# Attention's chain with one more fill point ahead of the latent, the scores and the last transposes; odd chunks 42 points behind even ones

## The chip, the cores and the metric

The kernel runs on one core of one Trainium2 chip. The metric is the device time of one execution in microseconds. Three runs of the kernel before gave 2309.78, 2309.92 and 2310.56 us; their median is 2309.92 us. A measurement of this kernel can tell a change of about 0.2%, some 4.6 us, from none.

## What is computed

Two layers over x of 8 sequences x 1024 tokens x 512 features, in float32, each with a layer norm ahead and a residual behind:

```python
x = x + attention(layernorm(x))
x = x + ffn(layernorm(x))

# attention
kv_latent = x @ W_to_kv.T                 # 512 -> 128
c  = kv_latent @ W_compress.T             # 128 -> 64
ch = layernorm(c) * gamma + beta
q  = rope(ch @ W_q.T);  k, v = split(ch @ W_kv.T);  k = rope(k)
o  = softmax(causal(q @ k.T / 8)) @ v     # one head of 64
z  = o @ W_comp2lat.T
out = z @ W_to_kv + z @ W_out_res.T + b

# ffn
hidden = silu(x @ W1.T) * (x @ W3.T)      # 512 -> 2048
out = fwht(hidden) @ W2.T                 # Walsh-Hadamard, 2048 -> 512
```

## The kernel before

**Tiling.** A sequence is cut into two chunks of 512 tokens; chunks are numbered a = 0 to 15, the even one is the first half of a sequence. A chunk has four tiles of 128 tokens. Every product is made of high and low parts (float16 or rounded float32), hence pairs and triples of matmuls. The attention of the two first chunks is done ahead of the main loop, in an order written out by hand.

**Main loop.** It runs over k = 0 to 127: sequence s = k // 16 and block h = k % 16 of the feed-forward's hidden features. Each k has seven products i = 0 to 6 of six matmuls each (`product`, L767 to L769; a seven-product scheme for the 2x2 block product). Behind products 1, 3, 5 and 6 TensorE does a `down` step (L791 to L793, six matmuls) for the second feed-forward matmul of four blocks before. VectorE and ScalarE turn the seven products into the hidden features: `copy_b` (ScalarE, behind product 0), `copy_p5` (behind 1), `sum_c` (VectorE, behind 2, needs copy_p5), `silu` 0 (ScalarE, behind 3), `sum_e` (VectorE, behind 4), `silu` 1 (behind 5), `hidden` 1 (VectorE, behind silu 1), `hidden` 0 (behind product 6 and silu 0), `high` (ScalarE, behind both hidden) and `low_part` (VectorE). Product (k, 2) waits for copy_b, (k, 4) for sum_c, (k, 6) for sum_e, (k+1, 1) for hidden 1. ScalarE does high(k-1) ahead of copy_b(k). `out_rows` (VectorE) takes a finished down tile to the output rows.

**Fill points.** While sequence s goes through the feed-forward, the attention of sequence s + 1 is laid into the same loop. After each product (and its down step) is a fill point f = 7h + j, j = 0 to 6. There every engine asks `SLOTS.get(f)`, which names the slot that each of the two chunks is at: the even chunk's slot is f - 3, the odd one's f - 3 - `ODD`. Each engine has a function `attention(a, slot)` that does its part of the slot. Every engine runs in its own order of instructions, so what stands in front of an attention step on an engine delays it, and the step delays what stands behind. Where a step falls among the engine's own work of the block is set by j: on ScalarE, point 0 lies between copy_b and copy_p5, 1 and 2 between copy_p5 and silu 0, 3 and 4 between the two silus, 5 and 6 behind silu 1 and ahead of high; on VectorE, 0 and 1 lie behind low_part of the block before and ahead of out_rows and sum_c, 2 and 3 between sum_c and sum_e, 4 ahead of hidden 1, 5 and 6 behind it and out_rows and ahead of hidden 0 (in every fourth block point 6 goes behind hidden 0 and high).

**The slots of a chunk before.** 0 to 3: `conv` (ScalarE L939, VectorE L1393) splits a block of x transposed; SP loads two more. 1 to 4: `cproj` on TensorE (L502, L503), the compression products; their source has one buffer, so conv and cproj go in turn. 5: `latent`: ScalarE copies the product (L945), TensorE turns it (L515), ScalarE copies the result (L951). 6: `squares`. 7, 8: statistics of x. 9 to 11: `norm1`, its Newton steps, `norm1_parts` (V, L1437). 13: `values`. 14: `proj`. 14 to 17: `rope`, ending with Q (L1475). From slot `TILE0` = 18 on come four tiles, 6 slots apart in an even chunk and 8 in an odd one: `scores` (L556) and `maxima` at +0, `exps` (ScalarE, L983, and its copies to high, L988) at +1, `low` (VectorE, L1496) at +2, transposes (L571, copied out by ScalarE, L999) at +4, `pv` (L586) at +5, `outp` (L596) one or two later, VectorE's part of it at +7. An odd chunk's tiles have 5 to 8 blocks of 128 keys, an even one's 1 to 4. Behind the last tile (`end_slot`): `norm2` at +1, `norm2_root` (nine small Newton operations, L1364 to L1368) at +2, `xnorm` from +3 and `xtrans` (L605, copied out by L1009) from +4.

`exps` needs another function table on ScalarE than `silu`; an ACT_TABLE_LOAD stands ahead of each change.

Two PSUM banks, X and Y, serve all attention steps of both chunks. In sequence 0 the loop carries more: the W1 and W3 forms are scaled and split (`scale_rows` on bank Y, L728; `forms_high` on ScalarE; `forms_low`), W2 is transformed (`hadamard2`, L719; `split2`), and there are no down steps in the first four blocks. `SCALE_AT` sets the points of scale_rows, moved by one where `y_held` says that a tile holds Y. SP issues loads and stores at fixed points and at slots: `load_x` at slot 3, the next chunk's `load_xT` at slot 36.

Of the kernel before, what the change touches and what calls it, by code (L numbers as in the profile page):

```python
# [16 lines left out]
NC = 16  # L17
# [22 lines left out]

ODD = 41
TILE0 = 18
NSLOT = 57
SLOTS = {z + 3: [(c, z - ODD * c) for c in range(2) if 0 <= z - ODD * c < NSLOT] for z in range(ODD + NSLOT)}


def y_held(f):

    return any(slot - TILE0 in ((0, 8, 16, 24) if c else (6, 12, 18, 24)) for c, slot in SLOTS.get(f, []))

# [76 lines left out]
def build_kernel(nc, x, xT, w13, w13t, w2, small, cst, tab, wscr, w2scr, w2tmp, out):  # L131
    with ExitStack() as ctx:
# [192 lines left out]
        def _(sp):  # L325
# [84 lines left out]
            def attention(a, slot):  # L410
                if slot in (0, 1):
                    load_xT(a, slot + 2)
                if slot == 3 and a > 1:
                    load_x(a)
                if slot == 36 and a + 1 < NC:
                    load_xT(a + 1, 0)
                    load_xT(a + 1, 1)

# [36 lines left out]
            for k in range(NK):  # L455
                s, h = divmod(k, NH)
                for j in range(7):
                    if s + 1 < NS:
                        for c, slot in SLOTS.get(7 * h + j, []):
                            attention(2 * s + 2 + c, slot)  # L460
                    if s and j == 0 and 1 <= h <= 4:
                        store(s - 1, 2 * h - 2)
                    if s and j == 3 and 1 <= h <= 4:
                        store(s - 1, 2 * h - 1)
                    if j == 2 and k % 4 == 0 and k >= 8:
                        load_w2s(k // 4)
                    if s == 0 and j == 3 and 1 <= h < NH - 1:
                        store_forms(h + 1)
                    if s == 0 and j == 6 and h < NH - 3:
                        load_raw(h + 3)  # L470
                    if s == 0 and 7 * h + j in SPLIT_END:
                        i = SPLIT_END[7 * h + j]
                        if i < 2:
                            load_half(i + 2)
                        store_w2(i)
                if NH <= k + 2 < NK:
                    load_forms(k + 2)
# [9 lines left out]
        def _(pe):  # L487
# [121 lines left out]
            def attention(a, slot):  # L609
                if 1 <= slot <= 4:  # L610
                    cproj(a, slot - 1)
                if slot == 5:
                    latent(a)
                if slot == 13:
                    values(a)
                if slot == 14:
                    proj(a)
                for t in range(4):
                    at = slot - tile_slot(a, t)
                    if at == 0:  # L620
                        scores(a, t)
                    if at == 4:
                        trans(a, t, 0)
                    if at == 5:
                        pv(a, t, 0)
                        if a % 2:
                            trans(a, t, 1)
                    if at == 6 and a % 2:
                        pv(a, t, 1)
                    if at == 5 + groups(a):  # L630
                        outp(a, t)
                    if slot == end_slot(a) + 4 + t:
                        xtrans(a, t)


# [263 lines left out]
            for k in range(NK):  # L899
                s, h = divmod(k, NH)  # L900
                for i in range(7):
# [3 lines left out]
                        down(4 * k + (1, 3, 5, 6).index(i) - 1)  # L905
                    f = 7 * h + i
                    if s + 1 < NS:
                        for c, slot in SLOTS.get(f, []):
                            attention(2 * s + 2 + c, slot)
                    if s == 0 and f in SCALE_AT:  # L910
                        scale_rows(SCALE_AT[f])
# [10 lines left out]
        def _(ac):  # L922
# [88 lines left out]
            def attention(a, slot):  # L1011
                if slot < 4:
                    conv(a, slot)
                if slot == 5:
                    latent(a)
                    latent2(a)
                if slot == 13:
# [5 lines left out]
                for t in range(4):  # L1023
# [6 lines left out]
                        trans(a, t, 1)  # L1030
                    if at == 4 + groups(a):
                        parts_o(a, t, oh, ol)
                    if slot == end_slot(a) + 4 + t:
                        xtrans(a, t)


# [267 lines left out]
            def fill(k, j):  # L1304
                s, h = divmod(k, NH)
                f = 7 * h + j
                if s + 1 < NS:
                    for c, slot in SLOTS.get(f, []):
                        attention(2 * s + 2 + c, slot)
                if s == 0 and f in SCALE_AT:  # L1310
                    scale_rows(SCALE_AT[f])
                if s == 0 and f in SPLIT_AT:
                    split2(SPLIT_AT[f])
# [43 lines left out]
        def _(ve):  # L1357
# [185 lines left out]
            def attention(a, slot):  # L1543
                if slot < 4:
                    conv(a, slot)
                if slot == 6:
                    kept["squares"] = squares(a)
                if slot == 7:
                    xstats(a, (0, 1))
                if slot == 8:  # L1550
                    kept["stats"] = xstats(a, (2, 3))
# [16 lines left out]
                for t in range(4):  # L1568
# [6 lines left out]
                        low(a, t)  # L1575
                    if at == 4 + groups(a):
                        parts_o(a, t, X[:, 0:128], oh, ol)
                    if slot == end_slot(a) + 3 + t:
                        xnorm(a, t)
                if slot == end_slot(a) + 1:  # L1580
                    norm2(a)
# [312 lines left out]
            def fill(k, j):  # L1894
                s, h = divmod(k, NH)
                if s + 1 < NS:
                    for c, slot in SLOTS.get(7 * h + j, []):
                        attention(2 * s + 2 + c, slot)
                f = 7 * h + j
                if s == 0:  # L1900
# [58 lines left out]
        def _(gp):  # L1959
# [53 lines left out]
            for k in range(NK):  # L2013
                s, h = divmod(k, NH)
                for j in range(7):
                    f = 7 * h + j
                    if s + 1 < NS:
                        for c, slot in SLOTS.get(f, []):
                            attention(2 * s + 2 + c, slot)
                    if s == 0:  # L2020
                        if j == 0 and 1 <= h < NH - 1:
# [55 lines left out]
```

## Time and profile before

| | us |
|---|---|
| median of three runs | 2309.92 |
| the profiled execution | 2304.87 |
| its span | 2303.1 |
| TensorE busy in the span | 2184.0 |
| VectorE busy | 1441.8 |
| ScalarE busy | 1049.9 |
| GpSimd busy | 230.8 |

The span runs from the first to the last instruction of the profiled execution, which is 5 us shorter than the median of the runs. Its mean granted TensorE clock is 0.982 of full speed. The main loop begins 113.0 us into the span; sequences 1 to 7 begin at 425.8, 695.7, 967.4, 1237.6, 1507.6, 1777.6 and 2047.5 us. In the profile a line number names the code, "out<-in" the tensors, and "idle before <-" what the engine waited for. Matmuls overlap: one of 512 columns lasts 0.38 us in the records, while the next begins 0.22 us after it.

### The profile page before, as it was taken

The page shows a single profiled execution, that of the slowest core. Times are in us where ns is not written, and L with a number is a line of the kernel's source. Part 1 is how long each engine was busy: PE and PEld are TensorE (multiplying, and loading weights), DVE is VectorE, ACT ScalarE, POOL GpSimd, SP SyncE. Part 2 cuts the span into 40 slices and gives each one's busy share as a digit, 9 for nine tenths or more (in the row PEclk, how much of TensorE's full clock was granted, in tenths as well). Part 3 has the DMA queues.
Part 4 walks back from the last instruction along what each step waited for, and adds up shares of the span by engine and source line. Part 5 has one row for each costly group of instructions (what it writes and reads, how often), then busy time and mean ns, then how long its engine had stood idle before and what let it go on. Part 6 is the DMA issues. An engine that isn't in the chain of part 4 may idle for free. (4 is left out here: it accounts for less than half of the span.)

```text
span 2303.1 us, 28485 instructions
## 1 busy us (share of the span) xinstructions
PE 2184.0 (95%) x10676; PEld 1051.1 (46%) x10676; DVE 1441.8 (63%) x2742; ACT 1049.9 (46%) x1577; POOL 230.8 (10%) x212
## 2 busy tenths in 40 slices
PE   6768899999999999999999999999999999999999
PEld 3424444444444444444444444544444444444444
DVE  7876766757557565665656665575656666563333
ACT  6746455354543535435444445435354354532221
POOL 2244444000000000000000000000000000000000
PEclk8799999999999999999999999999999999999999
DMA  8434322332223222233123321233222331123221
GB/s 323 154 124 161 110 94 85 126 112 94 69 72 133 94 90 78 82 118 111 67 85 111 119 83 68 83 112 110 94 76 77 109 128 67 67 92 110 83 83 53
DMA packets 59562, 236.50 MB, mean 103 GB/s; under 512 B 6433, under 2 KB 6561, under 8 KB 54049
## 3 DMA queue, kind: packets, MB, share of 16 engines
q1 hardware_dynamic: 59424, 234.68, 29.1%
q8 instruction: 85, 1.39, 0.2%
q14 instruction: 53, 0.43, 0.1%
HBM read 194.81 MB, written 39.85 MB: 102 GB/s over the span
## 5 line engine op out<-in xcount | busy, mean ns | idle before, releaser
L767 PE MATMUL PF<-XF,WS 128*128 128x512 f16 x1792 | 686.0, 383 | 16.9 <-DVE PF L1733 7.1
L768 PE MATMUL PF<-XF,WS 128*128 128x512 f16 x1792 | 684.4, 382 | 0.0
L769 PE MATMUL PF<-XF,WS 128*128 128x512 f16 x1792 | 683.6, 381 | 0.0
L791 PE MATMUL PD<-W2S,H 128*128 128x512 f16 x1024 | 389.3, 380 | 2.0 <-DVE H L1755 2.0
L792 PE MATMUL PD<-W2S,H 128*128 128x512 f16 x1024 | 389.1, 380 | 0.0
L793 PE MATMUL PD<-W2S,H 128*128 128x512 f16 x1024 | 388.9, 380 | 0.0
L1150 ACT ACTIVATE SH<-PF,afs 128x512 f32<-128x512 f32 x256 | 175.9, 687 | 360.6 <-PE PF L769 359.6
L767 PEld LDWEIGHTS PF<-XF,WS 128*128 128x128 f16 x1792 | 177.0, 99 | 229.1 <-issue 39.1
L1158 ACT ACTIVATE H<-SH 128x1024 f16<-128x1024 f32 x128 | 135.2, 1056 | 306.2 <-DVE SH L1747 306.2
L1747 DVE SCALAR_TENSOR_TENSOR SH<-PF,afs,SH 128x512 f32<-128x512 f32 x256 | 191.6, 748 | 132.7 <-ACT SH L1150 109.7
L769 PEld LDWEIGHTS PF<-XF,WS 128*128 128x128 f16 x1792 | 176.4, 98 | 214.6 <-issue 5.5
L768 PEld LDWEIGHTS PF<-XF,WS 128*128 128x128 f16 x1792 | 176.5, 99 | 171.9 <-issue 8.4
L1755 DVE TENSOR_TENSOR H<-SH,H 128x1024 f16<-128x1024 f32 x128 | 156.7, 1225 | 131.8 <-ACT H L1158 131.7
L1766 DVE SCALAR_TENSOR_TENSOR ring<-PD,afs,ring 128x512 f32<-128x512 f32 x224 | 166.8, 744 | 52.2 <-PE PD L793 52.1
L1966 POOL TENSOR_TENSOR ring<-ring,bb 128x512 f32<-128x512 f32 x56 | 71.7, 1307 | 1261.0 <-DVE st L1398 1241.3
L1737 DVE TENSOR_TENSOR PF<-PF,p 128x512 f32<-128x512 f32 x128 | 89.1, 696 | 166.0 <-PE PF L769 164.6
L791 PEld LDWEIGHTS PD<-W2S,H 128*128 128x128 f16 x1024 | 100.6, 98 | 124.7 <-issue 2.7
L792 PEld LDWEIGHTS PD<-W2S,H 128*128 128x128 f16 x1024 | 100.5, 98 | 121.9 <-issue 1.9
L793 PEld LDWEIGHTS PD<-W2S,H 128*128 128x128 f16 x1024 | 100.4, 98 | 121.5 <-issue 1.1
L1733 DVE TENSOR_TENSOR PF<-PF,p 128x512 f32<-128x512 f32 x128 | 88.7, 693 | 35.3 <-PE PF L769 34.6
L999 ACT ACTIVATE PT<-XY 128x1024 f16<-128x1024 f16 (+2 forms) x84 | 67.9, 809 | 82.7 <-PE XY L571 82.6
L1144 ACT ACTIVATE p<-PF 128x512 f32<-128x512 f32 x128 | 75.2, 588 | 34.2 <-PE PF L769 33.1
(312 smaller groups left out, 2368.8 us busy)
## 6 DMA issues: line engine op xcount, KB each, us to landing
WS<-wscr SPq DMA_DIRECT2D x112, 896.0 KB, 4.6
W2S<-w2scr SPq DMA_DIRECT2D x30, 1024.0 KB, 4.8
xraw<-xT SPq DMA_DIRECT2D x58, 256.0 KB, 4.6
ring<-x SPq DMA_DIRECT2D x56, 256.0 KB, 4.4
wscr<-WS SPq DMA_DIRECT2D x16, 896.0 KB, 3.7
out<-ring SPq DMA_DIRECT2D x56, 256.0 KB, 4.3
XF<-w SPq DMA_DIRECT2D x16, 512.0 KB, 8.6
RAW<-w13t SPq DMA_DIRECT2D x16, 512.0 KB, 4.5
```

What stands on the lines that cost most here:

```text
L767: pe.matmul(bank, wh, th, start=i < 2 and j == 0, stop=False, skip_group_check=True)
L768: pe.matmul(bank, wh, tl, start=False, stop=False, skip_group_check=True)
L769: m = pe.matmul(bank, wl, th, start=False, stop=j == 1, skip_group_check=True)
L791: pe.matmul(PD[:, t % 2, :], th, wh, start=j == 0, stop=False)
L792: pe.matmul(PD[:, t % 2, :], th, wl, start=False, stop=False)
L793: m = pe.matmul(PD[:, t % 2, :], tl, wh, start=False, stop=j == 3)
L1150: ac.activation(SH[:, i, :], PF[:, (1 - k % 2, 2)[i], :], ACT.Silu, scale=afs[:, k % NH:k % NH + 1]).then_inc((a_sb, a_sc2)[i], 1)
L1158: ac.activation(H[:, q % 2, k % 4, 0, :], SH[:, :, :].rearrange("p i c -> p (i c)"), ACT.Copy).then_inc(a_hi, 1)
L1737: ve.tensor_tensor(PF[:, 3, :], PF[:, k % 2, :], p5[:, :], ALU.add).then_inc(v_e, 1)
L1747: ve.scalar_tensor_tensor(SH[:, i, :], PF[:, (k % 2, 3)[i], :], afs[:, 16 + h:17 + h], SH[:, i, :], ALU.mult, ALU.mult).then_inc((v_hA, v_ ...
L1755: ve.tensor_tensor(H[:, q % 2, k % 4, 1, :], SH[:, :, :].rearrange("p i c -> p (i c)"), H[:, q % 2, k % 4, 0, :], ALU.subtract).then_inc(v ...
L1766: ve.scalar_tensor_tensor(row, PD[:, t % 2, :], afs[:, 65:66], row, ALU.mult, ALU.add).then_inc(v_ev, 1)
```

## The change

The even chunk's slots begin at the same fill point as before in sequences 1 to 6 and one point later in sequence 0 (the loop's sequence s = 0, which carries chunks 2 and 3). The odd chunk begins 42 points behind the even one, not 41. Within a chunk, the latent goes from slot 5 to 6 and squares from 6 to 7; the tiles begin at slot 19, not 18, so that everything from the scores on is one slot later; norm2 and norm2_root follow with the tiles; xnorm and xtrans are one slot later still. The load of the next chunk's xT goes from slot 36 to 37. `y_held`, and with it `SCALE_AT`, are worked out from the new slots. Conv, cproj, the statistics, norm1, values, proj and rope keep their slots.

```diff
--- before.py
+++ after.py
@@ -40,15 +40,20 @@
 
 
 
-ODD = 41
-TILE0 = 18
-NSLOT = 57
-SLOTS = {z + 3: [(c, z - ODD * c) for c in range(2) if 0 <= z - ODD * c < NSLOT] for z in range(ODD + NSLOT)}
+ODD = 42
+TILE0 = 19
+NSLOT = 59
+
+
+def slots(s, f):
+
+    z = f - (4 if s == 0 else 3)
+    return [(c, z - ODD * c) for c in range(2) if 0 <= z - ODD * c < NSLOT]
 
 
 def y_held(f):
 
-    return any(slot - TILE0 in ((0, 8, 16, 24) if c else (6, 12, 18, 24)) for c, slot in SLOTS.get(f, []))
+    return any(slot - TILE0 in ((0, 8, 16, 24) if c else (6, 12, 18, 24)) for c, slot in slots(0, f))
 
 
 
@@ -412,7 +417,7 @@
                     load_xT(a, slot + 2)
                 if slot == 3 and a > 1:
                     load_x(a)
-                if slot == 36 and a + 1 < NC:
+                if slot == ODD - 5 and a + 1 < NC:
                     load_xT(a + 1, 0)
                     load_xT(a + 1, 1)
 
@@ -456,7 +461,7 @@
                 s, h = divmod(k, NH)
                 for j in range(7):
                     if s + 1 < NS:
-                        for c, slot in SLOTS.get(7 * h + j, []):
+                        for c, slot in slots(s, 7 * h + j):
                             attention(2 * s + 2 + c, slot)
                     if s and j == 0 and 1 <= h <= 4:
                         store(s - 1, 2 * h - 2)
@@ -609,7 +614,7 @@
             def attention(a, slot):
                 if 1 <= slot <= 4:
                     cproj(a, slot - 1)
-                if slot == 5:
+                if slot == 6:
                     latent(a)
                 if slot == 13:
                     values(a)
@@ -629,7 +634,7 @@
                         pv(a, t, 1)
                     if at == 5 + groups(a):
                         outp(a, t)
-                    if slot == end_slot(a) + 4 + t:
+                    if slot == end_slot(a) + 5 + t:
                         xtrans(a, t)
 
 
@@ -905,7 +910,7 @@
                         down(4 * k + (1, 3, 5, 6).index(i) - 1)
                     f = 7 * h + i
                     if s + 1 < NS:
-                        for c, slot in SLOTS.get(f, []):
+                        for c, slot in slots(s, f):
                             attention(2 * s + 2 + c, slot)
                     if s == 0 and f in SCALE_AT:
                         scale_rows(SCALE_AT[f])
@@ -1011,7 +1016,7 @@
             def attention(a, slot):
                 if slot < 4:
                     conv(a, slot)
-                if slot == 5:
+                if slot == 6:
                     latent(a)
                     latent2(a)
                 if slot == 13:
@@ -1030,7 +1035,7 @@
                         trans(a, t, 1)
                     if at == 4 + groups(a):
                         parts_o(a, t, oh, ol)
-                    if slot == end_slot(a) + 4 + t:
+                    if slot == end_slot(a) + 5 + t:
                         xtrans(a, t)
 
 
@@ -1305,7 +1310,7 @@
                 s, h = divmod(k, NH)
                 f = 7 * h + j
                 if s + 1 < NS:
-                    for c, slot in SLOTS.get(f, []):
+                    for c, slot in slots(s, f):
                         attention(2 * s + 2 + c, slot)
                 if s == 0 and f in SCALE_AT:
                     scale_rows(SCALE_AT[f])
@@ -1543,9 +1548,8 @@
             def attention(a, slot):
                 if slot < 4:
                     conv(a, slot)
-                if slot == 6:
+                if slot == 7:
                     kept["squares"] = squares(a)
-                if slot == 7:
                     xstats(a, (0, 1))
                 if slot == 8:
                     kept["stats"] = xstats(a, (2, 3))
@@ -1575,7 +1579,7 @@
                         low(a, t)
                     if at == 4 + groups(a):
                         parts_o(a, t, X[:, 0:128], oh, ol)
-                    if slot == end_slot(a) + 3 + t:
+                    if slot == end_slot(a) + 4 + t:
                         xnorm(a, t)
                 if slot == end_slot(a) + 1:
                     norm2(a)
@@ -1894,7 +1898,7 @@
             def fill(k, j):
                 s, h = divmod(k, NH)
                 if s + 1 < NS:
-                    for c, slot in SLOTS.get(7 * h + j, []):
+                    for c, slot in slots(s, 7 * h + j):
                         attention(2 * s + 2 + c, slot)
                 f = 7 * h + j
                 if s == 0:
@@ -2015,7 +2019,7 @@
                 for j in range(7):
                     f = 7 * h + j
                     if s + 1 < NS:
-                        for c, slot in SLOTS.get(f, []):
+                        for c, slot in slots(s, f):
                             attention(2 * s + 2 + c, slot)
                     if s == 0:
                         if j == 0 and 1 <= h < NH - 1:
```

## Rows read from the trace of the kernel before

**Rows 1.** The page: busy line; a DMA issue line (KB, us to landing).

```profile
PE 2184.0 (95%) x10676; PEld 1051.1 (46%) x10676; DVE 1441.8 (63%) x2742; ACT 1049.9 (46%) x1577; POOL 230.8 (10%) x212
...
xraw<-xT SPq DMA_DIRECT2D x58, 256.0 KB, 4.6
```

**Rows 2.** Windows of sequences 0 and 3: length, busy by engine.

```profile
113.00:425.80 312.80, 272.09 (x1283) 129.14 (x1281) 217.81 (x385) 164.77 (x242) 139.61 (x133) 0.97 0.32 114
967.40:1237.60 270.20, 263.47 (x1321) 127.23 (x1320) 171.37 (x332) 123.56 (x179) 10.14 (x8) 0.99 0.27 94
```

**Rows 3.** Waits of TensorE in sequence 3: total us, times, longest.

```profile
PE XY L515 <- ACT PB L945: 2.2, 1, 2.2
PE XY L556 <- DVE Q L1475: 1.9, 2, 1.4
PE XY L502 <- DVE Kl L1393: 1.3, 3, 0.7
PE PF L767 <- DVE PF L1733: 0.7, 1, 0.7
PE XY L526 <- DVE V L1437: 0.4, 1, 0.4
```

**Rows 4.** Timeline before sequence 3's odd latent: start, us, what, idle.

```profile
1082.46 0.69 DVE L1393 TENSOR_TENSOR Kl<-xraw,Kh 128x512 fp32r<-128x512 f32 x1
...
1084.91 0.75 DVE L1747 SCALAR_TENSOR_TENSOR SH<-PF,afs,SH 128x512 f32<-128x512 f32 x1
...
1085.70 1.06 ACT L1158 ACTIVATE H<-SH 128x1024 f16<-128x1024 f32 x1 [3.79 <-DVE SH L1747]
...
1087.81 1.10 PE L515 MATMUL XY<-cst_s,PB 128*128 128x64 f32 x8 [2.25 <-ACT PB L945]
```

**Rows 5.** The window behind that latent; PEclk is third last.

```profile
1088.90:1092.40 3.50, 3.50 (x11) 1.24 (x9) 0.00 (x0) 0.98 (x2) 0.00 (x0) 0.52 0.00 0
```

**Rows 6.** Timeline around the scores of even tile 0, sequence 3.

```profile
1018.62 0.69 DVE L1475 TENSOR_TENSOR Q<-PB,Q 64x512 fp32r<-64x512 f32 x1 [0.69 <-ACT Q L975]
...
1019.37 0.38 PE L556 MATMUL XY<-Kh,Q 128*128 128x256 f32 x1 [1.45 <-DVE Q L1475]
...
1019.99 0.39 PE L767 MATMUL PF<-XF,WS 128*128 128x512 f16 x1
...
1021.09 0.58 ACT L1139 ACTIVATE PF<-PF 128x512 f32<-128x512 f32 x1
```

**Rows 7.** Timeline, odd tiles 0 and 2 of sequence 3.

```profile
1130.41 0.39 PE L571 MATMUL XY<-id,Ph 128*128 128x128 f16 x4
...
1162.56 0.39 PE L767 MATMUL PF<-XF,WS 128*128 128x512 f16 x1
...
1162.78 0.38 PE L768 MATMUL PF<-XF,WS 128*128 128x512 f16 x1
...
1164.31 1.01 ACT L983 ACTIVATE PB<-XY,st 128x896 f32<-128x896 f32 x1 [2.84 <-DVE st L1489]
...
1166.10 1.16 DVE L1496 SCALAR_TENSOR_TENSOR Pl<-PB,Ph 128x512 f16<-128x512 f32 x2 [0.54 <-ACT Ph L988]
...
1166.50 1.28 ACT L1150 ACT_TABLE_LOAD   x1
...
1167.79 0.69 ACT L1150 ACTIVATE SH<-PF,afs 128x512 f32<-128x512 f32 x1
...
1170.98 1.02 ACT L999 ACTIVATE PT<-XY 128x1024 f16<-128x1024 f16 x1 [1.05 <-PE XY L571]
```

**Rows 8.** Waits of TensorE in sequence 0, from 113.0 to 425.8.

```profile
PE XY L502 <- DVE Kl L1393: 7.0, 5, 3.3
...
PE XY L515 <- ACT PB L945: 5.6, 2, 2.9
...
PE XY L556 <- DVE Q L1475: 5.3, 2, 2.9
...
PE XY L526 <- DVE V L1437: 3.0, 2, 2.4
```

## The prediction

> **What bounds the kernel now.** I read the page's busy line first: TensorE is busy 2184.0 us of 2303.1 [rows 1], so the time is TensorE's work plus its pauses. The table of windows cuts the span at the first product of each sequence. Sequence 3 takes 270.20 us with 263.47 busy, so 6.7 us are pauses; sequence 0 has 40.7 us of them (312.80 - 272.09) [rows 2]. The windows of sequences 1, 2 and 4 to 6 are like that of 3; sequence 7 carries no attention and has no pause. The waits of TensorE inside sequence 3 name the pauses: 2.2 us at the latent, 1.9 at the scores in two, 1.3 at the compression products, 0.7 at a product, 0.4 at the values [rows 3]. These five are what a change of order can win; the products themselves cannot shrink.
>
> How a pause counts: product matmuls start every 0.22 us and last 0.38 [rows 7], so a pause of g costs about g + 0.16. A product or a down step is six of these, 1.30 us. Below, (h, j) is block h of 16 in a sequence, fill point j of 7, f = 7h + j. TensorE reaches j = 0 to 6 at 1.3, 3.9, 5.2, 7.8, 9.1, 11.7, 14.3 us of a block, plus what attention adds.
>
> The latent of the odd chunk is at (7,0). Its chain [rows 4, 6]: VectorE finishes the Newton steps of norm2_root at (6,6), then multiplies hidden (0.75), ScalarE copies high (1.06), copy_b (0.58), then the latent's own copy, and TensorE idles 2.25. The next window shows the second cost: from 1088.9 to 1092.4 TensorE is granted 0.52 of its clock, its 1.2 GHz level [rows 5]. Each of the six sequences has one such stretch right behind this wait (in sequence 2 it is twice as long). 3.4 us at half speed loses 1.7 us.
> The Trainium skill's "TensorE: Matmul & The Clock Gate" (Part 1: The HAM clock gate) says that the array is throttled unless activity releases it, and that idling brings the throttle back; by that rule, the trace agrees, and removing the pause removes the slow stretch too.
>
> **The change, part by part, sequences 1 to 6.** Fill points are added in front of three steps, and odd chunks move by one more. Nothing is computed more or less; every cost is a wait gained or lost.
>
> (a) Latent. Even: (1,1) to (1,2). Odd: (7,0) to (7,2), and norm2_root moves to (7,0), out of hidden's way, while norm2 and the last conv share (6,6). I replay the chain with the row durations, block 6 starting at 0. TensorE does the third compression product till 17.95; ScalarE's part of the last conv (a copy of copy_b's size, 0.6) and VectorE's (0.69, L1393 [rows 4]) end at 19.5; hidden 20.25, high 21.3, copy_b 21.9; product (7,2) starts at 22.75, so it doesn't wait. copy_p5 ends at 22.5, the latent's copy at 23.1, and TensorE arrives at 24.05. The wait is gone with 0.9 us to spare: 2.25 + 0.16 = 2.4 won, and 1.7 of clock. Next late is the chain of compression products: odd ones now fall on (6,4), (6,5), (6,6), (7,0), of which the last step leaves one product (1.3) for 0.6 + 0.69 plus handovers. I get waits of 0.3, 0.15 and 0.3 against 0.35 now: 0.4 lost. The odd values at (8,2) come to the phase at which even ones wait 0.4 [rows 3], and the last xnorms share VectorE with the statistics: 0.3 lost.
>
> (b) Scores of even tile 0, (3,0) to (3,1). Q is ready at 1019.31 [rows 6]; TensorE would arrive one product and one down step later than now (1019.37 - 1.45 - 0.16 = 1017.76), at 1020.35, so 1.45 + 0.16 = 1.6 goes. But the wait covered another: hidden stands behind Q on VectorE, and copy_b ends at 1021.67 whatever is moved [rows 6]. Product (3,2) would now be wanted at 1020.35 + 0.62 (scores, from 1019.37 to 1019.99) = 1020.97, so 0.7 comes back. Net won 0.85.
>
> (c) Odd tile 0, (8,6) to (9,1): its wait of 0.45 goes (0.6). Its exponentials leave (9,0), where they hold up copy_p5, and its low part leaves (9,1), ahead of sum_c; the 0.7 of the product (9,4) [rows 3] goes with them (0.9). Even tile 2 takes a like place, scores (4,6), exponentials (5,0), low (5,1), with 384 columns for 640: replayed, sum_c lands 0.35 after product (5,4) wants it. Lost 0.35.
>
> (d) Odd tile 2 is the bad one: scores (11,1) to (11,3), exponentials (11,4), low (11,5). Let E be the start of the product behind the scores (at 1162.56 now [rows 7]). Exp starts at E + 1.75 and ends with its copies at E + 3.92, the table load for silu at E + 5.22, silu at E + 5.9 (now they stand before the first silu of the block, which has room). Behind silu on VectorE are queued hidden (0.75), an out_rows of like size, the low part (1.4 with its two small steps) and the second hidden: E + 9.6. Then high 1.06, copy_b 0.58, and only then the copy of the transposes, 1.02: E + 12.2. TensorE wants it after six groups of 1.30, eight transposes (0.44: four take 0.39, of which 0.16 is tail [rows 7]) and two more groups, at E + 10.8. Lost 1.4. Odd tile 3 by the same count misses by 0.2, tile 1 by 0.05. Bounds: 0 if VectorE slips low in earlier, 3 if every handover is late; I take the replay.
> A second rule bears here: the Trainium skill's "ScalarE: Activation LUTs" (What ACT_TABLE_LOAD costs) gives a switch 1283 ns and as much again for a drain, 2.66 us. The row agrees with the first part (1.28), but silu starts 0.01 us behind the load [rows 7]. With a drain of about 1.4 the sum would be 8 us longer.
>
> (e) At no cost: on SP's queue the next chunk's xT load goes from slot 36 to 37, still five fill points (about 12 us) ahead of the conv, against 4.6 us to land [rows 1]; stores and weight loads keep their points, and loads of x keep their slot. GpSimd's bias adds keep slots 8 and 9, long before outp. The last xtrans goes from (13,6) to (14,2) of the odd chunk's first tile, the last tile to (14,5), and the next tokens begin at (15,0); if that cover were missing, the copy (0.6) would show once a sequence.
>
> Sum for a sequence: won 2.4 + 1.7 + 0.85 + 0.6 + 0.9 = 6.45; lost 0.4 + 0.3 + 0.35 + 1.65 = 2.7; net 3.75. Six of them 22.5, and 1.7 for the longer stretch of sequence 2: 24.2.
>
> **Sequence 0** moves by one more point. Its waits [rows 8]: compression 7.0, latent 5.6, scores 5.3, values 3.0. The first compression product waits for a load that lands by its own time, so the shift wins about one product; later the chain of VectorE is as tight as before: 6 of 7.0 stay. The latent comes to j = 3, behind silu: I leave 2.0 of 5.6. Scores come two points later: 0.5 of 5.3. Values: norm1_root no longer stands before hidden, 1.2 of 3.0 stay. Won 11.2. Of its slow stretches behind such waits I count two gone, 3.4. Lost: tile 1 is here in tile 2's bad place, with the scaled weight forms (a copy of high's size, 1.06) on ScalarE besides, 2.1; tiles 2 and 3 and even tile 3 at (6,0), 1.4. The scale_rows move among Y's users: some new waits, some old ones gone, 0 (bounds -2 and +2). Net about 11, bounds 2 and 18.
>
> Together 35 us: the profiled execution's 2304.9 would be 2270, the median of the three runs, 2309.9, which lies 5 us over it, 2275.
>
> **Rivals.**
> 1. The slow stretches stay, because another pause of the new order (odd tile 2, or the three of the compression) takes the latent's part. For: three of four new pauses lie in one stretch. Against: the scores' wait of 1.45 has no slow stretch behind it, and no new pause is longer. 6 x 1.7 + 1.7 + 3.4 less won: 2290. Chance 0.15.
> 2. Odd tile 2's chain has slack that I don't see, and the others too: 6 x 1.65 + 3 more won, 2262. Chance 0.12.
> 3. The change does nothing for the latent: ScalarE's copy moves with TensorE's step, both to the same point, and wherever ScalarE is late there it stays late. Then 2.4 + 1.7 remain in each, 26 us with sequence 2's, and some 5 in sequence 0: 2306. Against: at (7,2) ScalarE has only copy_p5 ahead of it. Chance 0.05.
> 4. Slower: exponentials behind the first silu. All three of odd tiles 1 to 3 stand there now; each late silu delays hidden, high, copy_b and product 2 in turn. It decides once the three cost over 5.4 us a sequence together (6.45 less 1.05 of other losses) where I have 1.65; at 2.5 each with a slow stretch behind, 9.2, the sum is 3.8 x 6 = 23 lost and sequence 0 won by nothing: 2333. Chance 0.08.
> 5. The drain of the table switch shows in this place: 8 us less won, 2283, chance 0.02; the row speaks against it.
>
> **How the numbers follow.** My forecast has 0.58, the rest as above. It alone spans 2264 to 2288 (sequence 0's bounds, and 0 to 3 for tile 2). The range goes down past rival 2 and up past rival 1, 2258 to 2298, and leaves out rivals 3 and 4 and the far tails. A measurement here can tell about 0.2%, 4.6 us. Faster 0.58 + 0.15 + 0.12 + 0.02 = 0.87, same 0.05, slower 0.08.
>
> **What would show it.** Right: no wait at the latent in sequences 1 to 6 and a clock of 1.00 there; product (3,2) waiting 0.6 to 0.7 for copy_b; no wait at the scores; odd tile 2's pv or transposes waiting 1 to 1.4 at (12,0) or (12,1); PE idle per sequence 4 to 5 us with a length near 266. Wrong: slow clock in other places; a wait over 2 us anywhere in sequences 1 to 6; sequence 0 no shorter than 309.

## The result and the profile after

The changed kernel takes 2281.32 us (median of 4 runs, 2280.13 to 2282.66); the kernel before, run beside it, 2310.24 us. The ratio is 0.9875, with a 95% interval of 0.9858 to 0.9892: 1.25% faster, 29 us. The forecast was 2275, in a range of 2258 to 2298.

The page of the kernel after, its span and its busy line, which answers to [rows 1]:

```profile
span 2278.3 us, 28484 instructions
...
PE 2172.3 (95%) x10676; PEld 1046.4 (46%) x10676; DVE 1437.6 (63%) x2742; ACT 1045.2 (46%) x1577; POOL 231.7 (10%) x212
```

The span is 24.8 us shorter. TensorE runs the same 10676 matmuls and is busy 11.7 us less, since slow-clock matmuls count as longer ones; the other 13.1 us are pauses.

Windows of the kernel after: sequence 0, sequence 3, and the place behind the odd latent of sequence 3 (length, busy time by engine, granted clock third last); they answer to [rows 2, 5]:

```profile
112.90:426.40 313.50, 272.49 (x1282) 129.59 (x1280) 216.93 (x385) 163.76 (x243) 141.57 (x133) 0.97 0.32 114
957.90:1223.90 266.00, 261.68 (x1322) 126.65 (x1321) 170.87 (x332) 122.95 (x179) 9.99 (x8) 1.00 0.28 96
1079.00:1082.50 3.50, 3.50 (x22) 2.18 (x21) 2.34 (x7) 1.07 (x2) 0.00 (x0) 1.00 0.02 5
```

Sequence 3 went from 270.20 to 266.00, with 4.3 us of pauses for 6.7 and a clock of 1.00 where 0.52 stood. Sequences 1 to 6 begin at 426.4 and 692.1 and end at 2021.1 (425.8, 695.7 and 2047.5 before): 1594.7 us for 1621.7, **27.0 won**. Sequence 0 takes 313.5 for 312.8: **0.7 lost**. From sequence 7's start to the end it is 257.2 for 255.6: **1.6 lost**. Together 24.7, which is the span's 24.8 but for rounding. The medians lie 29 apart because the profiled execution before was 5.4 us under its median (2304.87 for 2310.24) and the one after 1.2 under its own (2280.13 for 2281.32).

Waits of TensorE in sequence 3 after (total us, times, longest), against [rows 3]:

```profile
PE XY L507 <- DVE Kl L1398: 1.5, 4, 0.7
PE PF L772 <- ACT PF L1144: 0.8, 1, 0.8
PE XY L610 <- DVE xs L1543: 0.8, 2, 0.6
PE XY L591 <- ACT PT L1004: 0.7, 1, 0.7
PE XY L531 <- DVE V L1442: 0.4, 1, 0.4
```

Latent, scores and the product that waited for sum_c (L1737 now) are gone from the list. New are product (3,2) behind copy_b, the last transposes behind xnorm, and odd tile 2's pv behind the copy of its transposes.

Waits of TensorE in sequence 0 after, against [rows 8]:

```profile
PE XY L507 <- DVE Kl L1398: 10.1, 4, 3.3
PE PF L772 <- ACT PF L1144: 7.8, 3, 5.6
PE PD L724 <- DVE W2S L1708: 5.6, 3, 3.9
...
PE XY L610 <- DVE xs L1543: 2.0, 1, 2.0
PE XY L591 <- ACT PT L1004: 1.9, 2, 1.0
PE XY L520 <- ACT PB L950: 1.3, 1, 1.3
```

Latent fell from 5.6 to 1.3, scores from 5.3 and values from 3.0 to nothing. Compression rose from 7.0 to 10.1, and W2's transform waits 5.6 for `split2`, which in the kernel before waited 0.8 in all:

```profile
PE PD L719 <- DVE W2S L1704: 0.8, 2, 0.6
```

### The profile page after: what moved, and what is told of

The parts are those of the page before. It is cut to its first block and busy times, and to the rows that moved or that the text cites. A ratio compares the mean times of both kernels' runs of the same rounds, so it can differ in the third digit from the quotient of the medians.

```text
span 2278.3 us, 28484 instructions
## 1 busy us (share of the span) xinstructions
PE 2172.3 (95%) x10676; PEld 1046.4 (46%) x10676; DVE 1437.6 (63%) x2742; ACT 1045.2 (46%) x1577; POOL 231.7 (10%) x212
## 5 line engine op out<-in xcount | busy, mean ns | idle before, releaser
L1737 DVE TENSOR_TENSOR PF<-PF,p 128x512 f32<-128x512 f32 x128 | 88.6, 692 | 32.2 <-PE PF L774 32.2
```

## The experiments

All have three rounds beside the kernel before. Its median was 2307.22 in the first four, 2308.04 in the next four and 2308.65 in the last four, so medians of different groups are a few us uncertain against each other, and "us faster" below is worked out from the ratio. The lengths of sequences 1 to 6 in the profiled executions tell smaller differences, since six alike stand in each. Sequence 0 stands there once: where two kernels have the same code in it, it took 310.7 and 310.7, 312.8 and 312.9, and 313.5 and 314.4 us, so a difference under 1 us in it says nothing. Only once, below, is a part added to the work; none leaves any out.

### The parts of the change, each alone

**Only the latent**, in the kernel before:

```diff
-                if slot == 5:
+                if slot == 6:
                     latent(a)
...
-                if slot == 6:
+                if slot == 7:
                     kept["squares"] = squares(a)
-                if slot == 7:
```

> The kernel before with the latent at slot 6 and squares at slot 7 alone; 41 and the tiles' slots as before. The odd latent then stands at (7,1). My account of the pause: ScalarE ends copy_b at about the same time, copy_p5 follows, then the latent's copy; TensorE arrives 2.6 us later than before, so the wait of 2.25 falls to 0.3 or less in sequences 1 to 6 and the slow clock behind it goes: 4 us a sequence, 24 to 26 us in all, 2285. If the slow clock doesn't hang on the pause: 14 us, 2296. If ScalarE stays as late as TensorE: 2310.

Measured: 2302.38, ratio 0.9972 (0.9960 to 0.9984), about 6 us faster and none of the three expected times. The latent still waits 1.17 at (7,1), and a slow-clock stretch of 3.4 us stands behind it in all six sequences.

**Only the odd chunks**, 42 behind:

```diff
-ODD = 41
+ODD = 42
...
-                if slot == 36 and a + 1 < NC:
+                if slot == 37 and a + 1 < NC:
```

> The kernel before with the odd chunk 42 points behind instead of 41, and the xT load at slot 37, nothing else. The odd latent at (7,1), norm2_root still at (6,6). If the place of the latent matters, most of its wait goes; the scores' wait of 1.45 on the even side stays, odd scores at (9,0) wait up to 1.5. I expect 2290 to 2300. If only the added slot ahead of the latent helps: 2308 to 2312.

Measured: 2311.63, ratio 1.0015 (1.0006 to 1.0025), 3.5 us slower. The second expected range has the time, but not for its reason: the latent's wait did fall, to 1.17, and new waits took more than that. The odd scores of tile 0, now at (9,0), wait 1.45 for Q where they waited 0.45, and odd tiles 2 and 3 wait 0.85 twice for the copy of their transposes and 0.42 once for the low part. Pauses are 8.0 us a sequence for 6.5 (sequence 1). The timeline around the odd latent of sequence 3 in this kernel (start, us, engine, line, operation, what, idle before and what ended it):

```profile
1086.30 0.75 DVE L1747 SCALAR_TENSOR_TENSOR SH<-PF,afs,SH 128x512 f32<-128x512 f32 x1
...
1089.31 0.54 DVE L1538 TENSOR_SCALAR xs<-ring,st 128x512 f32<-128x512 f32 x1
...
1089.91 0.66 PE L605 MATMUL XY<-cst_s,xs 128*128 128x128 f32 x4
...
1090.60 0.60 ACT L1009 ACTIVATE XS<-XY 128x512 f32<-128x512 f32 x1 [1.46 <-PE XY L605]
...
1091.10 0.59 ACT L945 ACTIVATE PB<-XY 128x512 f32<-128x512 f32 x1
...
1091.74 0.43 PE L515 MATMUL XY<-cst_s,PB 128*128 128x64 f32 x2 [1.17 <-ACT PB L945]
```

What holds up the latent now stands in these rows: the even chunk's first xtrans stands at (7,1), the point to which the odd latent has moved. The even chunk comes first at a point, so ScalarE's copy of the latent is queued behind the copy of the transposes (L1009), which waits 1.46 for TensorE. The latent by its slot alone comes to the same point; there the same queue stands.

**Only the tiles**, one slot later:

```diff
-TILE0 = 18
-NSLOT = 57
+TILE0 = 19
+NSLOT = 58
```

> The kernel before with the tiles from slot 19 on and all behind them one slot later; latent, 41 and xtrans's distance to the tiles as before. Even scores win 1.6 and product (3,2) gives back 0.7 to 0.9; norm2_root moves from (6,6) to (7,0), so hidden 0 of block 6 is 2 us earlier and the latent at (7,0) waits only 0.3 to 0.8 instead of 2.25, with no slow clock. I expect 3 to 5 us a sequence, 2285 to 2295. The rival, that the tiles' move is worth the scores alone: 2304 to 2308.

Measured: 2299.38, ratio 0.9964 (0.9951 to 0.9977), 8 us faster, between the two expected ranges. The odd latent still waits 1.67 at (7,0), but only once (544.1) with a slow stretch behind it. The pauses did not shrink: they are 7.0 us a sequence for 6.5, with 0.79 new at the compression products and 2.1 at odd tiles 2 and 3. What sequences 1 to 6 gain, 3.6 us (1618.1 for 1621.7), is clock.

The three alone make -6.5, +3.5 and -8.3, together -11; the whole change makes -29. So parts of it work only in company: the later tiles take norm2_root and the even xtrans away from the odd latent, and the 42 points give it room. The next experiment says which. A fourth part, the last xnorm and xtrans one slot later still, was not run by itself.

**The changed kernel with the latent put back** to slot 5 and squares to 6 (the edit of the first experiment, reversed):

> The changed kernel with the latent back at slot 5 and the squares at 6; the odd chunks stay 42 behind and the tiles one later. Nothing is left out. If the latent's own move is what takes the wait away, the odd latent waits 1.2 to 2.2 us again in each of sequences 1 to 6 (1.17 with 42 behind alone, 1.67 with the later tiles alone, 2.24 in the kernel before), partly with the slow clock behind it (0 to 1.7 us each): 7 to 20 us slower than the changed kernel, 2288 to 2301. If the 42 points and the later tiles have already taken most of it, under 4 us slower.

Measured: 2275.39, ratio 0.9859 (0.9844 to 0.9874), not slower at all. The wait that was expected back did not come; the last sentence of the expectation, under 4 us slower, holds. Timeline around the odd latent of sequence 3, first in this kernel:

```profile
1072.99 0.58 ACT L1144 ACTIVATE PF<-PF 128x512 f32<-128x512 f32 x1
...
1073.51 0.58 ACT L1149 ACTIVATE p<-PF 128x512 f32<-128x512 f32 x1
...
1073.98 0.58 ACT L950 ACTIVATE PB<-XY 128x512 f32<-128x512 f32 x1
...
1074.62 1.10 PE L520 MATMUL XY<-cst_s,PB 128*128 128x64 f32 x8
```

and in the kernel after:

```profile
1074.80 0.74 DVE L1751 SCALAR_TENSOR_TENSOR SH<-PF,afs,SH 128x512 f32<-128x512 f32 x1
...
1077.54 0.58 ACT L950 ACTIVATE PB<-XY 128x512 f32<-128x512 f32 x1
...
1079.41 0.78 PE L520 MATMUL XY<-cst_s,PB 128*128 128x64 f32 x6
```

With the latent at (7,1), TensorE arrives 0.06 us behind the end of the copy (1073.98 + 0.58 to 1074.62) and doesn't wait; at (7,2) it arrives 1.29 behind it. So the other parts had already taken the wait. The latent's own move costs: sequences 1 to 6 are 265.35 long without it and 265.8 with it, 2.6 us in all, and the wait of 0.6 at xtrans (7,5) is 0 without it. The rest of the span's 7.1 us is sequence 0 (310.6 for 313.5) and the end (255.6 for 257.2).

### The slow clock

**The pause filled.** Kernel before; eight matmuls of 512 columns, whose result nobody reads, go into the latent's bank ahead of the odd latent's wait:

```diff
-                w.wait_ge(a_cT, one(a))
                 w.wait_ge(d_cst, 16)
                 if a > 1:
                     w.wait_ge(*yfree)
+                if a > 3 and a % 2:
+                    for r in range(8):
+                        pe.matmul(b, id16[:, :], V[:, 0:4, :].rearrange("p k c -> p (k c)"), start=True, stop=True)
+                w.wait_ge(a_cT, one(a))
```

> The kernel before with eight idle-time matmuls (128x512, 1.73 us by the 0.22 us start to start) put on TensorE ahead of the odd latent's wait of 2.25, in chunks 5 to 15, into the bank that the latent overwrites; their result is not used. They add work and remove no wait of the chain: the latent still starts when its copy is done. If the slow clock behind this wait comes from TensorE's idling there, the six slow stretches go and the kernel is 10 to 12 us faster with 48 matmuls more. If the slow clock has another cause, the time stays or grows by up to 1.

Measured: 2296.65, ratio 0.9958 (0.9943 to 0.9972), 10 us faster by the ratio; the five runs lie between 2294.41 and 2302.57. Timeline and window of this kernel at the odd latent of sequence 3:

```profile
1083.00 1.89 PE L515 MATMUL XY<-V,id 128*128 128x512 f16 x8
...
1085.42 1.10 PE L518 MATMUL XY<-cst_s,PB 128*128 128x64 f32 x8 [0.52 <-ACT PB L948]
...
1085.40:1092.40 7.00, 6.98 (x40) 4.23 (x41) 3.46 (x8) 2.18 (x4) 0.00 (x0) 1.00 0.00 0
```

The copy comes no sooner, so the latent is not sooner; what is gone is only the slow stretch, in all six sequences: 6 x 1.7 + 1.7 = 11.9 expected from the rows, 10.8 measured in sequences 1 to 6 (1610.9 for 1621.7). That the pause brings the 1.2 GHz level is thereby shown for this place. The Trainium skill has the slow level come back when TensorE idles, in "TensorE: Matmul & The Clock Gate" (Part 1: The HAM clock gate); the trace agrees here: 0.52 behind the pause, 1.00 with the pause filled.

### Sequence 0

**Sequence 0 not shifted**, in the changed kernel:

```diff
-    z = f - (4 if s == 0 else 3)
+    z = f - 3
```

> The changed kernel with sequence 0's slots one point earlier again (even chunk at f - 3 as in all other sequences); the 42, the latent, the tiles and the last transposes stay as changed. In the changed kernel sequence 0 took 313.5 us, no less than before (312.8). If the extra point of sequence 0 is what ate its gain, this is 5 to 10 us faster than the changed kernel. If the point only moves VectorE's small steps in and out of GpSimd's long operation, other waits come and the time is within 4 us of it, either way. Sequences 1 to 6 stay at 265.7 us each.

Measured: 2277.48, ratio 0.9869 (0.9855 to 0.9884); sequence 0 takes 310.7 for 313.5, and other steps wait in it (values 2.4, xtrans 3.0, W2's transform 4.2). The point of the start is worth 2.8 us in sequence 0, not 5 to 10; something else decides.

A part of it shows in the timeline of the kernel after, at (2,2):

```profile
168.39 0.16 DVE L1371 TENSOR_TENSOR st<-st 128x4 f32<-128x4 f32 x1
168.56 2.12 POOL L2001 TENSOR_TENSOR WS<-WX,WS 128x1024 f16<-128x1024 f32 x1 [4.63 <-ACT WS L1122]
168.59 2.12 DVE L1373 SCALAR_TENSOR_TENSOR st<-st 128x4 f32<-128x4 f32 x1
...
172.93 1.13 PE L724 MATMUL PD<-H,cst_s 128*128 128x512 f32 x2 [3.90 <-DVE W2S L1708]
```

and at (7,1):

```profile
263.83 2.12 POOL L2001 TENSOR_TENSOR WS<-WX,WS 128x1024 f16<-128x1024 f32 x1 [8.36 <-ACT WS L1122]
263.87 2.10 DVE L1532 TENSOR_SCALAR st<-st 128x4 f32<-128x4 f32 x1
...
267.24 0.80 PE L507 MATMUL XY<-Kh,Wc 128*128 128x512 f32 x1 [3.30 <-DVE Kl L1398]
```

A VectorE operation on four columns, 0.16 us elsewhere, lasts as long as GpSimd's low part of the weight forms beside which it starts: it ends when that ends. In sequence 0 of the kernel after five such small operations last over 0.5 us, 9.6 us together, four of them 2.0 to 2.1; before there were seven, 6.4 us together, none over 1.2. The longest of before, in its timeline:

```profile
277.95 1.20 DVE L1374 TENSOR_SCALAR sti<-st 128x4 int32<-128x4 int32 x1
```

The Trainium skill has this in "SBUF — State Buffer" (Who interferes with whom): VectorE and GpSimd share a pair of ports that one holds for a whole instruction, against VectorE operations with two SBUF inputs or in a two-port mode. The trace agrees: `split2` (L1708), which reads PSUM and one SBUF operand, takes 0.75 beside L2001 and 0.74 alone.

**GpSimd's operation in four pieces**, changed kernel:

```diff
-                gp.tensor_tensor(WS[:, h % 2, 1, 0:4, :], WF[:, 0:4, :], WS[:, h % 2, 0, 0:4, :], ALU.subtract).then_inc(g_wl, 1)
+                for f in range(4):
+                    i = gp.tensor_tensor(WS[:, h % 2, 1, f, :], WF[:, f, :], WS[:, h % 2, 0, f, :], ALU.subtract)
+                i.then_inc(g_wl, 1)
```

> The changed kernel with GpSimd's low part of the weight forms (one tensor_tensor of 1024 columns, 2.1 us, in sequence 0 only) cut into four of 256. In the changed kernel VectorE's small Newton and norm operations last 2.1 us instead of 0.16 three times in sequence 0, each time beside this one GpSimd operation, and TensorE then waits 3.9 at (2,2), 3.3 at (7,1) and 2.0 at (14,3). If the two engines exclude each other for the length of one GpSimd operation, each of these waits falls by 1.2 to 1.6 and the slow clock behind two of them goes: sequence 0 takes 305 to 309 instead of 313.5, 4 to 8 us in all. If these waits come from the added point's order alone: no change, within 1.

Measured: 2277.91, ratio 0.9872 (0.9857 to 0.9887), sequence 0 313.6 long: no gain in it, the 4 to 8 us missed. Timeline at (2,2):

```profile
167.66 2.55 POOL L2002 TENSOR_TENSOR WS<-WX,WS 128x256 f16<-128x256 f32 x4 [4.64 <-ACT WS L1122]
167.68 0.66 DVE L1373 SCALAR_TENSOR_TENSOR st<-st 128x4 f32<-128x4 f32 x1
168.38 0.59 DVE L1369 TENSOR_TENSOR st<-st 128x4 f32<-128x4 f32 x1
169.01 0.59 DVE L1371 TENSOR_TENSOR st<-st 128x4 f32<-128x4 f32 x1
169.63 0.59 DVE L1373 SCALAR_TENSOR_TENSOR st<-st 128x4 f32<-128x4 f32 x1
...
172.06 1.22 PE L724 MATMUL PD<-H,cst_s 128*128 128x512 f32 x1 [3.93 <-DVE W2S L1708]
```

Each piece holds up one small operation. Four dependent steps pass in the pieces' 2.55 us where one passed in 2.12, so three steps of 0.2 are saved and 0.43 is lost. The waits are 3.93 for 3.90 at (2,2), 3.05 for 3.30 at (7,1) and 1.79 for 1.95 at (14,3). The stand-still is there as said; cutting the long operation does not remove it.

**GpSimd's operation later**, changed kernel, behind VectorE's own low part, so behind all Newton steps of that point:

```diff
                         if j == 0 and 1 <= h < NH - 1:
+                            w.wait_ge(v_wl, h + 2)
                             forms_low(h + 1)
```

> The changed kernel in which GpSimd's low parts of the weight forms (L2001, 2.1 us each) start behind VectorE's own low parts (L1715) in sequence 0, where now they start with them. Nothing is left out. If the waits of sequence 0 come from VectorE's small operations standing still beside L2001 (one of 128x4 lasts 2.1 us instead of 0.16 at (2,2), (7,1) and (14,1)), the waits of 3.9 us at (2,2) and 3.3 at (7,1) fall by about 2 each and that of 1.95 at (14,3) by 1 to 2: sequence 0 falls from 313.5 to 307 to 309, the kernel to about 2276. If the forms behind it are what is late (L1990 and on start 1 to 2 us later each), the scaled forms are late for the next block and sequence 0 stays within 1.5 of 313.5 or grows.

Measured: 2273.51, ratio 0.9851 (0.9834 to 0.9867). Window of sequence 0, and the two places of above:

```profile
112.70:418.80 306.10, 271.46 (x1283) 128.95 (x1281) 206.90 (x385) 163.94 (x243) 136.97 (x133) 0.97 0.32 116
...
167.76 0.16 DVE L1373 SCALAR_TENSOR_TENSOR st<-st 128x4 f32<-128x4 f32 x1
...
170.02 1.12 PE L724 MATMUL PD<-H,cst_s 128*128 128x512 f32 x2 [1.81 <-DVE W2S L1708]
...
172.69 2.13 POOL L2001 TENSOR_TENSOR WS<-WX,WS 128x1024 f16<-128x1024 f32 x1 [9.59 <-DVE WS L1715]
...
264.02 0.49 PE L507 MATMUL XY<-Kh,Wc 128*128 128x512 f32 x1 [1.23 <-DVE Kl L1398]
```

Sequence 0 falls by 7.4 to 306.1, the waits by 2.1 each as expected, and VectorE is busy 10.0 us less (206.90 for 216.93) with the same work. Of the 7.4 us, 6.4 are pauses (41.0 to 34.6). One added wait on GpSimd gives back much of what sequence 0 had failed to win. But VectorE was busy 217.81 in sequence 0 of the kernel before, so it stood still there as much; the late forms were not tried in that kernel, and how much they would win there is not known.

### The new waits of sequences 1 to 6

**The bias add in four pieces**, changed kernel. xnorm (L1543) lasts 1.55 for 0.55 beside GpSimd's two adds of 1.25 each, and the last transposes wait for it, in the timeline of the kernel after at (7,5) of sequence 3:

```profile
1085.48 2.49 POOL L1970 TENSOR_TENSOR ring<-ring,bb 128x512 f32<-128x512 f32 x2 [95.76 <-DVE st L1403]
1086.71 1.55 DVE L1543 TENSOR_SCALAR xs<-ring,st 128x512 f32<-128x512 f32 x1
```

The edit:

```diff
-                    gp.tensor_tensor(xrow(a, t), xrow(a, t), bb[:, :], ALU.add).then_inc(g_bias, 1)
+                    for c in range(4):
+                        i = gp.tensor_tensor(xrow(a, t)[:, 128 * c:128 * c + 128], xrow(a, t)[:, 128 * c:128 * c + 128],
+                                             bb[:, 128 * c:128 * c + 128], ALU.add)
+                    i.then_inc(g_bias, 1)
```

> The changed kernel with GpSimd's bias add (512 columns, 1.27 us, four a chunk) cut into four of 128 columns. In the changed kernel xnorm lasts 1.55 instead of 0.54 beside it, and the last transposes wait 0.57 and 0.22 at (7,5) and (7,6). With the cut both waits should go or halve: 0.5 to 0.9 a sequence, 3 to 5 us in all. If xnorm is slow for another reason: no change. More instructions on GpSimd cost nothing there.

Measured: 2281.74, ratio 0.9885 (0.9869 to 0.9902); sequences 1 to 6 take 266.0. The wait at xtrans falls to 0.2, but the small operations of norm1, 0.16 before, now last 0.37 to 0.42 beside the pieces, and values waits 0.6 more in odd chunks. The wait moved, and the 3 to 5 us did not come. Sequence 0 took 316.3 for 313.5, with 32.9 us of slow clock for 20.5.

**`low` of odd tile 2 one point earlier**, so at (11,4) and ahead of hidden, changed kernel:

```diff
-                    if at == 2:
+                    if at == (1 if t == 2 and a % 2 and a > 3 else 2):
                         low(a, t)
```

> The changed kernel with the low part of odd tile 2 one point earlier on VectorE, at (11,4) and not (11,5), from chunk 5 on. VectorE then stands idle for the copies of the exponentials before it, but low is ahead of hidden 1, out_rows and hidden 0 instead of behind the first two. By my account of the queue (silu at E + 5.9, low ends at E + 5.4) hidden 0 ends 1.4 us earlier, and the waits of 0.2 at (12,0) and 0.9 at (12,1) go: 6 to 7 us in all. If high and copy_b are not what is late there: no change, or up to 3 slower by VectorE's idling ahead of sum_e.

Measured: 2275.85, ratio 0.9861 (0.9846 to 0.9875). Timelines of sequence 3, first of the kernel after, then of this one:

```profile
1158.90 1.15 DVE L1501 SCALAR_TENSOR_TENSOR Pl<-PB,Ph 128x512 f16<-128x512 f32 x2
...
1163.56 0.62 PE L591 MATMUL XY<-PT,V 128*128 128x128 f16 x8 [0.71 <-ACT PT L1004]
```

```profile
1154.06 1.16 DVE L1501 SCALAR_TENSOR_TENSOR Pl<-PB,Ph 128x512 f16<-128x512 f32 x2 [1.22 <-ACT Ph L993]
...
1161.33 0.61 PE L591 MATMUL XY<-PT,V 128*128 128x128 f16 x8
```

Sequences 1 to 6 take 264.65 each, 1.1 less and 6.8 in all; the waits at (12,0) and (12,1) are both gone, as expected. So low behind hidden and out_rows, as the prediction had queued it, is what made pv late.

### Together

**Low early and sequence 0 not shifted:**

> The changed kernel with two edits that were each tried alone: low of odd chunks' tile 2 one point earlier (alone 2275.85), and sequence 0 not shifted (alone 2277.48). Nothing is left out. If they add up: 1.1 us less in each of sequences 1 to 6 and 2 to 3 less in sequence 0 with its even scores' stage unshifted, so 2272 to 2274, ratio 0.984. If sequence 0 is only rearranged by anything that moves in it, as its waits suggest, 2274 to 2277.

Measured: 2270.11, ratio 0.9833 (0.9819 to 0.9848); sequences 1 to 6 take 264.7 each and sequence 0 310.7, each as in the kernel with that edit alone. The two add up.

**These and GpSimd's forms late:**

> The two edits of the kernel before this in the list and the late low forms of GpSimd together. If VectorE's stand-still beside L2001 is a cause of sequence 0's waits in any arrangement, it is 3 to 5 us faster than the same kernel without them, about 2269. If the wait only trades places, it is within 1.5 us of it.

Measured: 2267.38, ratio 0.9823 (0.9808 to 0.9837), the lowest median of all, 1.8% faster than the kernel before and some 12 us faster than the changed one by the ratios (0.9875 - 0.9823 = 0.0052). It is 2.7 us under the kernel without the late forms, between the two expectations and within what the runs can tell. Sequence 0 is 309.4 for 310.7. Its pauses fell by the expected amount, from 39.4 to 35.8, but TensorE was busy 2.3 us longer (273.6 for 271.3), with 21.3 us of slow clock for 17.1. Unshifted, only one of the long small operations stood beside L2001 (2.12), and what remained stands beside the bias adds, five of 1.2 to 1.3. The late forms with the shift gave 306.1 for sequence 0; low early, late forms, the shift and the latent at slot 5 together were not run.

## Why the prediction was right, and where it was not

The forecast of 2275 was 6 us low. In the profiled executions, from which it was worked out, the change wins 24.7 of the 35 us forecast, so it was 10 low there; 4 of these are hidden in the medians by how far each profiled execution lay under its own. That the forecast came so near is in part luck. By its own steps, in us of the profiled executions:

| | predicted | measured |
|---|---|---|
| sequences 1 to 6 | -24.2 | -27.0 |
| sequence 0 | -11 | +0.7 |
| the rest | 0 | +1.6 |

**(a) Latent, 2.4 + 1.7.** Right: no wait, clock 1.00, 1.29 us to spare where 0.9 was counted. What the step did not say is which edit does it. It replayed the chain for the new point with its new neighbours and got the right end, but with the latent back at its old slot the wait is gone as well: the other parts do the whole, and the latent's own move loses 0.4 a sequence.

**The slow clock** went from sequences 1 to 6 altogether, and rival 1, another pause taking its part, didn't come: the largest wait is now 0.8. The drain of rival 5 didn't show either: silu starts at 1156.86, 0.02 us behind the end of the table load (1155.56 + 1.28) in sequence 3.

**(b) Even scores.** Won as said; the product's wait for copy_b came back as 0.79, 0.95 with the 0.16, for 0.7.

**(c)** Odd scores and product (9,4) are gone as said. Product (5,4) doesn't wait, for 0.35 counted.

**(d) Odd tile 2**, 1.4 counted: 0.2 at the transposes and 0.9 at pv, 1.1; tiles 1 and 3, 0.25 counted, nothing. The experiment with an earlier low took exactly this away.

**(a), the rest.** Odd compression lost 0.4 as counted: it waits 0.2 at (6,4) and 0.2 at (7,0), 0.7 a sequence with 0.16 for each, where it cost 0.35. Odd values lost nothing and xnorm 1.1 (0.7 at (7,5), 0.4 at (7,6)), where 0.3 stood for both: the term was mis-sized because VectorE's xnorm was priced at its own 0.54, not at 1.55 beside GpSimd, whose bias adds (e) had put among the things at no cost. Against this 0.8 too little, and 0.2 in (b), stand 0.35 + 0.3 + 0.25 too much in (c) and (d). Added up so, the net would be about 3.7; 3.75 was counted, and the lengths give 4.2, (27.0 - 1.7) / 6. The last 0.5 was not traced.

**Sequence 0: the failed step.** "Net about 11" came from halving the waits of [rows 8] line by line. The three lines that were to fall fell further than counted: latent, scores and values 13.9 to 1.3 where 3.7 were left. But of compression 10.1 stayed, where 6 were counted, W2's transform went from 0.8 to 5.6, and xtrans from 0.5 to 2.0. Nor did the clock help: two slow stretches were counted gone, 3.4, but 20.5 us of slow clock stand in sequence 0 for 17.1, 6.8 of them from 266.2 on, at the compression's wait of 3.3. Taken together, pauses were to fall by 7.7 and rose by 0.3, and TensorE's busy time was to fall by 3.4 and rose by 0.4. The step took VectorE's small steps at 0.16 wherever they fell and never asked what GpSimd does at that moment. In sequence 0 it works 141.57 of 313.5 us; the new order set the small steps beside its longest instruction four times. That they delay TensorE there, the late forms show: -7.4 with nothing else touched. Of the 11.7 missed that would leave 4.3, of which 1.6 are pauses and 2.7 TensorE's busy time, the slow stretches that did not go. What is not shown is that all of the 7.4 belongs to the new order: in the kernel before VectorE was busy as long, and the late forms were not run there. Of the prediction's signs of being wrong this one came: sequence 0 no shorter than 309.

**The rest.** The last group of down steps waits 1.98 for low_part in both kernels; after, 3.4 us of slow clock (2252.7) follow it, before none did. That was not in the sum: 1.6.

## What to carry to other kernels

When an order is shifted, list what else stands at the point where each moved step lands, on every engine: here two edits alone each put a copy into the same queue behind another chunk's transposes and took only half of its wait, and the edit that moved the transposes away made one of the two needless. Price a small VectorE step by what GpSimd runs beside it, not by its own row, and where the two meet, move the long GpSimd instruction behind the chain instead of cutting it. A pause of TensorE is worth more than its length when a slow-clock stretch follows it; look in the windows behind the pause, and count both.

## What the runs showed of the hardware that was not expected

- Work that nobody reads made a kernel faster: with 48 more matmuls sequences 1 to 6 took 10.8 us less, all of it from the clock.
- Like pauses are not always followed by the slow level. A latent wait of 1.17 us had a slow stretch behind it in six of six sequences in one kernel (only the latent; there a wait of 0.38 stands 1.8 us ahead of it) and in one of six in another (only the odd chunks). One of 1.67 had it in one of six (only the tiles). A scores wait of 1.45 had none at (3,0), in six sequences of the kernel before, and one in three of six at (9,0) (only the odd chunks). The tail's 1.98 had one in the changed kernel and none in the same kernel with sequence 0 unshifted. What else decides was not found. A slow stretch lasted 3.4 us in most places of the main loop, 6.8 or 10.2 in some.
- The exclusion between GpSimd and VectorE goes by instruction: four columns wait out a whole operation of 1024 (0.16 becomes 2.12), and against four pieces of 0.67 each small operation waits out one piece (0.59 to 0.66).
